# A fused GNN kernel: where the walk over edge tiles gets its block and ring slot numbers

## What is computed

```python
# third layer (attention, 2 heads of 64)
qi = q[tgt]; kj = k[src] + e; vj = v[src] + e
alpha = jnp.sum(qi * kj, axis=-1) / math.sqrt(C)
amax = jax.ops.segment_max(alpha, tgt, num_segments=n)
ex = jnp.exp(alpha - amax[tgt])
den = jax.ops.segment_sum(ex, tgt, num_segments=n)
agg = jax.ops.segment_sum((ex / (den[tgt] + 1e-08))[:, :, None] * vj, tgt, num_segments=n)
# fourth layer (messages)
msg = jax.nn.relu(jnp.concatenate([edge_feat, hid[src]], axis=1) @ W1 + b1)
msg_sum = jax.ops.segment_sum(msg, dst, num_segments=N_NODES)
```

## Time and profile before

| | |
|---|---|
| median of 3 runs | 3705.48 us |
| profiled execution: span | 4103.0 us |
| PE busy | 3139.2 us (77%), 17480 matmuls |
| DVE, ACT, POOL busy | 1986.4, 1606.3, 1627.3 us |
| attention, first to last gather | 1644.0 to 2888.6 us; its walk ends at 2998 |
| messages, first to last gather | 3064.3 to 4005.3 us; its walk ends at 4069 |

### The profile page before, as it was taken

The page is one execution under the profiler, slowest core; times in us unless marked ns, Lnnn a source line. Parts: engine busy times, 40 slices in busy tenths (PEclk is TensorE's granted clock), DMA queues, the critical chain, the costliest instruction groups (busy, mean ns, idle before and its releaser), DMA issues. The chain is left out here.

```text
span 4103.0 us, 80080 instructions
## 1 busy us (share of the span) xinstructions
PE 3139.2 (77%) x17480; PEld 1972.5 (48%) x17480; DVE 1986.4 (48%) x6935; ACT 1606.3 (39%) x4621; POOL 1627.3 (40%) x1766
## 2 busy tenths in 40 slices
PE   3788788879997797577777777777866778787877
PEld 2444444444443343455566656556643444444445
DVE  6656666556656115344444444444673444444442
ACT  1555555413322001233333333333453444444445
POOL 2000000024333001666666666666106666666660
PEclk7899898999998998687777777877977888888885
DMA  1111111125557995322222222222112222222220
GB/s 38 57 59 57 57 59 59 51 93 193 188 177 261 406 360 185 65 54 55 54 55 54 55 54 53 54 55 54 40 28 56 66 63 66 64 66 63 66 61 13
DMA packets 417722, 370.64 MB, mean 90 GB/s; under 512 B 175608, under 2 KB 342232, under 8 KB 417336
## 3 DMA queue, kind: packets, MB, share of 16 engines
q1 hardware_dynamic: 365912, 315.65, 23.8%
q0 software_dynamic: 46144, 48.98, 6.5%
q10 hardware_dynamic: 5280, 1.23, 0.1%
HBM read 279.65 MB, written 86.00 MB: 89 GB/s over the span
## 5 line engine op out<-in xcount | busy, mean ns | idle before, releaser
L1451 POOL DMA_INDIRECT big<-row_table,src x806 | 761.5, 945 | 487.3 <-issue 183.4
L1870 POOL DMA_INDIRECT big<-message_table,src x610 | 612.0, 1003 | 394.5 <-DVE big L2000 172.1
L1476 PE MATMUL banks<-big 97*128 x902 | 399.8, 534 | 148.6 <-issue 138.1
L1492 PE MATMUL banks<-big 128*128 x1804 | 349.0, 326 | 174.8 <-ACT big L1508 110.1
L486 PE MATMUL banks<-work 128*128 128x226 f16 x1197 | 350.3, 293 | 138.6 <-issue 131.0
L1492 PEld LDWEIGHTS banks<-big 128*128 128x128 f32 x1804 | 312.4, 244 | 202.5 <-issue 202.1
L1909 PE MATMUL banks<-big 128*128 128x512 f16 x1225 | 395.6, 441 | 4.4 <-DVE big L1988 4.4
L850 PE MATMUL banks<-big,work 128*128 128x512 f16 (+1 forms) x1750 | 352.1, 359 | 22.3 <-DVE work L984 17.4
L1541 DVE TENSOR_REDUCE big<-banks 128x1 f32<-128x256 f32 x451 | 189.4, 420 | 332.5 <-PE banks L1476 183.8
L1508 ACT COPY big<-banks 128x256 f32<-128x256 f32 x451 | 169.8, 377 | 439.5 <-remote 194.0
L1918 PEld LDWEIGHTS banks<-big 128*64 128x64 f32 x1804 | 173.8, 164 | 343.6 <-issue 343.0
(11 more groups left out here) (338 smaller groups left out, 5835.8 us busy)
## 6 DMA issues: line engine op xcount, KB each, us to landing
big<-weights_halves SPq DMA_DIRECT2D x16, 6400.0 KB, 20.8
weights_dense<-work SPq DMA_DIRECT2D x196, 200.0 KB, 1.9
work<-weights_dense SPq DMA_DIRECT2D x196, 200.0 KB, 2.7
weights_halves<-work SPq DMA_DIRECT2D x98, 400.0 KB, 2.6
big<-q_table SPq DMA_DIRECT2D x451, 64.0 KB
big<-in_ef SPq DMA_DIRECT2D x403, 64.0 KB
big<-in_ea SPq DMA_DIRECT2D x403, 32.0 KB
big<-row_table,src POOLq DMA_INDIRECT x806
```

The lines of the kernel that those rows point to most:

```text
L1451: po.indirect_dma_start(rows[:, t % RT, s, 0:D], None, x_t.rearrange("a p c -> (a p) c"), bass.IndirectOffsetOnAxis(ap=m.src2[:, s, t:t + ...
L1476: pe.matmul(psS[v % 2], qT[v % R][0:XW, :], XF[0:XW, bass.ds(slot, 1), :].rearrange("p t e -> p (t e)"), start=False, stop=True).then_inc( ...
L1492: ins = pe.matmul(psA[v % 2], PT[v % 2][:, s * P:(s + 1) * P], rows[:, bass.ds(slot, 1), s, :].rearrange("p t c -> p (t c)"), start=(s == ...
L1870: po.indirect_dma_start(G[n % R][:, s, :], None, g_t.rearrange("a p c -> (a p) c"), bass.IndirectOffsetOnAxis(ap=m.src2[:, s, t:t + 1], ax ...
```

## The change

`stage_tables` writes two tables of 16 bit integers, the block and the ring slot of each visit, one value a visit, instead of one table of packed words. `Walk` replaces `Blocks`: one register load brings sixteen values, unchecked, and `of(v)` is one of the sixteen registers. SyncE and DVE walk the block table, TensorE the slot table.

```diff
-BLOCK1, ENDS, BLOCK2 = 0, 32, 96
+BLOCK1, ENDS, BLOCK2, SLOT2 = 0, 32, 64, 96
-NWORDS = V2P // 4
-WORDS = 2
+LEG = 16
...
-            own = valid[BLOCK2:BLOCK2 + 1, 0:V2P]
-            chain(dve.tensor_scalar(own, j2[BLOCK2:BLOCK2 + 1, :], float(J2 - 1), None, ALU.min))
-            four = own.rearrange("p (k u) -> p k u", u=4)
-            word = tmp[BLOCK2:BLOCK2 + 1, 0:NWORDS]
-            chain(dve.scalar_tensor_tensor(word, four[:, :, 3], float(JPAD), four[:, :, 2], ALU.mult, ALU.add))
-            chain(dve.scalar_tensor_tensor(word, word, float(JPAD), four[:, :, 1], ALU.mult, ALU.add))
-            chain(dve.scalar_tensor_tensor(m.blocks2(), word, float(JPAD), four[:, :, 0], ALU.mult, ALU.add))
+            own, tile2 = valid[:, 0:V2P], tmp[:, 0:V2P]
+            tileI = jI[:, 0:V2P]
+            chain(dve.tensor_scalar(own, j2, float(J2 - 1), None, ALU.min))
+            chain(dve.tensor_tensor(tile2, iotaF[:, 0:V2P], own, ALU.subtract))
+            chain(dve.tensor_copy(tileI, tile2))
+            chain(dve.tensor_scalar(tileI, tileI, RT - 1, None, ALU.bitwise_and))
+            chain(dve.tensor_copy(m.slots2(), tileI[SLOT2:SLOT2 + 1, :]))
+            chain(dve.tensor_copy(m.blocks2(), own[BLOCK2:BLOCK2 + 1, :]))
...
-class Blocks:
-    def __init__(self, nc, m, eng):
-        self.nc, self.m, self.eng = nc, m, eng
-        self.loaded, self.first = {}, 0
+class Walk:
+    def __init__(self, nc, table, eng, most):
+        self.nc, self.table, self.eng, self.most = nc, table.bitcast(U16), eng, most
+        self.loaded = {}
     def of(self, v):
-        g = v // (4 * WORDS)
+        g = v // LEG
         if g not in self.loaded:
-            n = min(WORDS, NWORDS - g * WORDS)
-            _, xs = self.nc.values_load_multi_w_load_instructions(self.m.blocks2()[:, g * WORDS:g * WORDS + n], [self.eng], min_val=0,
-                                                                  max_val=JPAD ** 4 - 1)
+            n = min(LEG, V2P - g * LEG)
+            _, xs = self.nc.values_load_multi_w_load_instructions(self.table[:, g * LEG:g * LEG + n], [self.eng], min_val=0, max_val=self.most,
+                                                                  skip_runtime_bounds_check_because=BOUNDED)
             self.loaded = {g: xs, **{k: x for k, x in self.loaded.items() if k == g - 1}}
-        u = v % (4 * WORDS)
-        return (self.loaded[g][u // 4] >> (6 * (u % 4))) & (JPAD - 1)
-    def slot(self, v):
-        return (v + RT - self.of(v)) & (RT - 1)
+        return self.loaded[g][v % LEG]
+def blocks(nc, m, eng):
+    return Walk(nc, m.blocks2(), eng, J2 - 1)
+def slots(nc, m, eng):
+    return Walk(nc, m.slots2(), eng, RT - 1)
...
-            own = Blocks(nc, m, mybir.EngineType.PE)
+            own = slots(nc, m, mybir.EngineType.PE)
...
-                    slot = own.slot(v)
+                    slot = own.of(v)
```

More of the change, by code:

```diff
@@ L12 @@
 I16 = mybir.dt.int16
+U16 = mybir.dt.uint16
 ALU = mybir.AluOpType
@@ L66 @@
 NDC = -(-NDST // DC)
-BLOCK1, ENDS, BLOCK2 = 0, 32, 96
+BLOCK1, ENDS, BLOCK2, SLOT2 = 0, 32, 64, 96
 R = 8
 RT = 64
-NWORDS = V2P // 4
-WORDS = 2
+LEG = 16
+BOUNDED = "the table is written from values that are clamped when it is made"
 FAR = 1 << 20
@@ L154, in blocks2, with slots2 @@
     def blocks2(self):
-        return self.vis[BLOCK2:BLOCK2 + 1, :].bitcast(I32)[:, 0:NWORDS]
+        return self.vis[BLOCK2:BLOCK2 + 1, 0:V2P]
+    def slots2(self):
+        return self.vis[SLOT2:SLOT2 + 1, 0:V2P]
     def counts(self):
@@ L1430, in _ @@
         def _(sp):
-            own = Blocks(nc, m, mybir.EngineType.SP)
+            own = blocks(nc, m, mybir.EngineType.SP)
             for v in range(V2):
@@ L1524, in _ @@
             dve.wait_ge(init, 1)
-            own = Blocks(nc, m, mybir.EngineType.DVE)
+            own = blocks(nc, m, mybir.EngineType.DVE)
             def onehot(v, s):
```

## The result

The new kernel takes **3719.42 us** (5 runs, 3712.12 to 3726.74), against 3705.66 for the kernel before (5 runs): ratio 1.003, 95% interval 1.0016 to 1.0044. The forecast of 3684 us and its range up to 3708 were wrong, and so was the direction. A second comparison (e5) gives 1.0023 (1.0014 to 1.0032), so a slowdown of 0.2 to 0.3% was measured twice.

The account below looks back on a forecast made before the run. POOL's gathers were taken to bound the first 403 steps of each walk, so only the last 48 would gain: -17 (attention) - 6 (messages) + 1.5 (tables) = -21.5 us, from 3705.5 to 3684 us. The range was 3640 to 3708.

Parts of the forecast that it names:

- What bounds the kernel: Both walks: POOL's gathers, 2.50 us a tile, bound the first 403 steps; TensorE needs 2.06 us with a new tile.
- delays of the recording: POOL's waits beyond 0.30 us a gather, 245.5 us in attention and 146.9 in messages, were taken as profiling delays.
- The gathering steps: First 403 steps of each walk: POOL's list doesn't change, so the change saves 0 us.
- Attention's last 48 steps: Plain step 1.72 to 1.44 us, sixteen-value load 0.66 us: 17 us saved in three rounds, ends 10 and 25.
- the third rival: Both walks' last 48 steps: load time (L) grows with its values, 4.3 us each; +23 us, 3728; chance 0.10.
- I am wrong the other way if TENSOR_LOAD takes microseconds: Register load of sixteen values: stated sign of failure, against the expected time near 0.66 us.
- The other end of the bounds: Register load in attention's last 48 steps: time in proportion to the values, 0.269 us each, 4.3 us for sixteen.
- The messages' last 48 steps: ACT's 6.9 us for eight steps is the next bound: 6 us saved, at most 7, or nothing.
- The tables: Table stage on DVE: four small instructions become six of 460 elements, +1.5 us, between +0.8 and +2.3.
- The checks: TensorE's register loads: two run time checks of 0.15 us each go, 0.3 us a load.
- The first rival: Gathering steps not at POOL's pace throughout: with a quarter at TensorE's pace, 56 us more goes, 3628; chance 0.17.
- the second: TensorE's idle 0.28 us a step only makes room for another wait, so nothing comes out: 3703; chance 0.13.

Follow-up runs that it names:

- e5: The new kernel unchanged, measured again in a second comparison with the kernel before: 3711.61 us, ratio 1.0023.
- e13: The kernel before, unchanged, profiled again: profiled execution 3704.05 us, span 3702.3 us.
- e7: The kernel before with one of each tile's two indirect DMAs, the second half of its rows left zero: 3289.7 us, ratio 0.8875.
- e9: The new kernel with one of each tile's two indirect DMAs, the second half of its rows left zero: 3376.4 us, ratio 0.9112 to the kernel before.
- e12: The kernel before, unchanged, profiled again: 4138.75 us.
- e14: The new kernel with eight 16 bit values a register load in place of sixteen: 3701.3 us, ratio 0.9981 to the kernel before.
- e6: The new kernel with both tables as 32 bit words, eight a load: 3674.0 us, ratio 0.9921 to the kernel before.
- e10: The new kernel with both tables as 32 bit words, four a load: 3668.4 us, ratio 0.9905 to the kernel before.
- e2: The new kernel with both tables as 32 bit words, sixteen a load: 4048.16 us, ratio 0.9849 to the kernel before, which took 4110.5 us there.
- e11: The kernel before with only the run time checks of the packed words left out: 3692.5 us, ratio 0.9969.
- e3: The new kernel with both tables as 32 bit words, eight a load: 4047.0 us, ratio 0.9843 to the kernel before, which took 4110.5 us there.

## Why the prediction was wrong, step by step

- **What bounds the kernel: right.** POOL sets the pace of both walks' first 403 steps at the level of 3705 us (e13; e7 to e9). TensorE's step with a new tile was put at 2.06 us, and e7 shows 1.90. What was wrong is the reason given for the 400 us between profile and runs: they aren't delays of the recording, since the profiled execution of e12 took 4138.75 us and another of the same kernel beside it 4137.64, while e13, recorded as well, took 3704.05. The long register operations belong to that level too: 839 ns at most in the first trace, 48 in e13. What the POOL waits come from there is open.
- **The gathering steps, 0: right in attention** (1005.4 against 1006.0 us). In the messages they took 5.9 us more, all in the gathers themselves (mean 1004 against 995 ns, 610 of them). e14 has the same 1004, e6 and e10 have 1000 and 998. Why these gathers last longer isn't settled.
- **Attention's last 48 steps, -17: the failed step.** The failed term is the 0.66 us for a load of sixteen 16 bit values; it measured 3.79 and 3.59. The other term was good: a plain step is 1.33 us, not 1.44. The formula of the third rival, 23.0 + 2L - 0.4 for a leg, gives 30.0 at L = 3.7, and 29.55 was measured. With short loads (e6) the last 48 steps fell by 20.8 us, within the ends of 10 and 25. The prediction had named the sign itself: "I am wrong the other way if TENSOR_LOAD takes microseconds". How the error came about: the two rows were 537 ns for two words and 591 for eight, and I drew a line through them. But two words aren't on the line of full groups of four (333, 591, 1106 ns for 4, 8, 16), and neither row had 16 bit values. The other end of the bounds, 0.269 us a value, was nearly the truth (0.233), and it was taken from the same row of 537; the text even names that the rows were "32 bit values". The width of a value decided (e2), and it deserved more than 1 in 10.
- **The messages' last 48 steps, -6:** they fell by 1.7, and with short loads by 9.8, more than the 7 taken as the most; a step of e6 takes 0.81 us there in the mean, less than the 0.86 that I took from the earlier trace rows as ACT's pace.
- **The tables, +1.5: right.** From L382 (now L387) to the large additions of the next stage, L447 (now L453), it takes 5.72 us in place of 4.49, 1.2 more.
- **The checks were under-priced:** 0.3 us a load on TensorE alone, where 1.03 came out (e11), since they follow each other on two engines. Of the 36 us that e10 gains, e11 has 12.
- **The rivals.** The third, long loads, is what happened, and it was right for attention. At L = 3.7 it gives 3 x 4.7 + 1.5 = +15.6 us, 3721, and 3719.4 and 3711.6 were measured; that this comes so near is in part luck. 12.6 of its 15.6 us are the messages' legs, put at 13.8 + 2L - 0.8 = 20.4 us each, and a leg took 16.3, as before: the two loads don't come on top of ACT's 13.8 us, since ACT goes on beside them. In its place 5.9 us came from the messages' gathers, which no term has. The first rival has POOL's idle time against it, the second e6.
- The Trainium skill, "Runtime: NRT & Kernel Launch", section "Instruction fetch mechanics", puts a register load at about 200 ns a register even in bulk. The page says so of loads from HBM; here the values come from SBUF, which the prediction left out. For 16 bit values the runs come near it all the same (233 ns a value), and I dismissed it on rows of 32 bit words; for these it doesn't hold from four on, 1106 ns for sixteen being 69 each.

## What to carry to other kernels

Before trading instructions for a longer one, find a row of that very form, data type and length, or give the figure that speaks against you the weight of a bound: two rows of a kindred form fixed a line that wasn't there. In this kernel a table of ready values beats packed ones if the numbers that an engine's sequencer loads are 32 bit words, in multiples of four, and unchecked where the data are known to be in bounds. Where a slow producer hides all but the end of a loop, a change of its inner step is priced at the end alone: here 96 steps of 902.

## What the runs showed of the hardware

- A register load on TensorE takes about 0.08 us and 0.257 us for each four 32 bit words (e2, e6, e10); two words take 537 ns, more than four (333). 16 bit values cost 233 ns each on TensorE, 220 on DVE ((3588 - 1827) / 8).
- The Trainium skill, "DMA: Bandwidth & Descriptors", section "Latency and other measured facts", gives `tensor_load` a floor of about 600 ns; four words took 333 ns here (e10), below it.
- Three stops of TensorE for loads of some 3.8 us were each followed by a stretch at 1.2 GHz, and the granted clock of attention's tail was 0.88; with loads of 0.6 us it was 1.00 through the same steps (e6).
- The same kernel before ran at 3704 to 3707 us in some comparisons and at 4110 to 4139 in others, with POOL's waits in the two gather stages as nearly all of the difference (388 of 401 us between the spans of the first trace and e13). What sets the level is open. On the second level the eight words a load of e3 gain 63 us, on the first (e6) 30.
